# Exponents of a masked decay product in fp32r instead of bf16, in a two-layer attention kernel on one core

## The reference, cut to what matters

```
log_f = log_sigmoid(fg)                       # (8 heads, 128)
cs = cumsum(log_f, axis=1)
log_D = where(tril, cs[:, :, None] - cs[:, None, :], -inf) + ig[:, None, :]
D_mat = exp(log_D - max(log_D, -1))
C = (q k^T / sqrt(32)) * D_mat
h = (C / (max(|sum C|, exp(-max log_D)) + 1e-6)) v
```

## Time and profile before

| what | value |
|---|---|
| median of three runs | 572.49 us (571.02 to 572.50) |
| the profiled execution: time | 568.18 us |
| the profiled execution: span of its trace | 566.5 us |
| TensorE's mean granted clock in it | 0.994 of 2.4 GHz |
| stage A in it | 25.2 to 118.7 us |

### The profile page before, as it was taken

How to read it: one execution, slowest core, us unless ns; L and a number is a source line. 1 busy time by engine, 2 the same in 40 slices (tenths; PEclk the granted TensorE clock), 3 DMA queues, 4 the chain that set the end, 5 groups by cost and what they waited for, 6 DMA issues and landing times.

```text
span 566.5 us, 8464 instructions
## 1 busy us (share of the span) xinstructions
PE 547.5 (97%) x2773; PEld 447.2 (79%) x2773; DVE 326.7 (58%) x799; ACT 230.2 (41%) x436; POOL 71.2 (13%) x105
## 2 busy tenths in 40 slices
PE   7798998999999999899999999999999999999997
PEld 5566576679888888778888878888878889788887
DVE  6677789768877779773353463434552444542333
ACT  2344545647878844362121361122351122441111
POOL 5232324111412323100000000000000000000000
PEclk9998999999999999999999999999999999999999
DMA  7685537334986999200000100000100000000001
GB/s 206 161 199 175 99 105 185 91 118 169 363 303 204 198 318 229 78 1 0 1 0 1 37 2 1 0 1 0 37 1 1 1 1 19 20 1 0 1 0 39
DMA packets 59296, 47.69 MB, mean 84 GB/s; under 512 B 37278, under 2 KB 50590, under 8 KB 58852
## 3 DMA queue, kind: packets, MB, share of 16 engines
q1 hardware_dynamic: 54264, 30.39, 20.1%
q0 software_dynamic: 4848, 16.78, 9.1%
q10 hardware_dynamic: 148, 0.04, 0.0%
HBM read 40.58 MB, written 2.10 MB: 75 GB/s over the span
## 4 chain that ended last, share of the span: by engine, by line
PE 58%; issue 7%; POOL 2%; DVE 1%; POOLq 0%; DVEq 0%
PE ps L914 57%; POOL rstd L445 1%; POOL h L551 1%; PE ps L584 0%; PE ps L878 0%; DVE qr L1527 0%; DVE x L1515 0%; DVE xn L1275 0%; DVE alT L1554 0%; DVE xT L1282 0%; POOL w L540 0%; POOLq L551 0%; POOL w L542 0%; PE ps L869 0%; DVE ot L1607 0%
## 5 line engine op out<-in xcount | busy, mean ns | idle before, releaser
L914 PE MATMUL ps<-hBt,h 128*128 128x512 f32 x512 | 117.5, 390 | 0.0
L914 PE MATMUL ps<-hA,h 128*128 128x512 f32 x512 | 117.3, 390 | 0.0
L1238 ACT ACTIVATE h<-ps,scol 128x512 f32<-128x512 f32 x64 | 44.2, 690 | 175.3 <-PE ps L914 175.2
L914 PEld LDWEIGHTS ps<-hA,h 128*128 128x128 f32 x512 | 95.9, 188 | 20.4 <-DVE hA L1581 0.6
L914 PEld LDWEIGHTS ps<-hBt,h 128*128 128x128 f32 x512 | 95.8, 188 | 20.3 <-DVE hBt L1581 0.6
L914 PE MATMUL ps<-xT,w 128*128 128x512 f32 x256 | 61.7, 396 | 1.0 <-DVE xT L1282 1.0
L914 PEld LDWEIGHTS ps<-xT,w 128*128 128x128 f32 x256 | 46.2, 188 | 15.0 <-issue 6.0
L1599 DVE CAST hBt<-h 128x512 fp32r<-128x512 f32 x32 | 13.7, 427 | 73.7 <-ACT h L1238 73.7
L1599 DVE CAST hA<-h 128x512 fp32r<-128x512 f32 x32 | 13.7, 427 | 70.0 <-ACT h L1238 70.0
L445 POOL TENSOR_TENSOR rstd<-ve,mhalf 128x4 f32<-128x4 f32 x16 | 16.7, 1041 | 262.9 <-DVE ve L1270 262.9
L1221 ACT ACTIVATE silD<-ps,scol 128x512 f32<-128x512 f32 x32 | 22.1, 689 | 45.2 <-PE ps L914 45.2
(11 more groups left out here) (174 smaller groups left out, 877.2 us busy)
## 6 DMA issues: line engine op xcount, KB each, us to landing
looked<-w_all_in SPq DMA_DIRECT2D x16, 704.0 KB, 5.6
h<-w_all_in POOLq DMA_DIRECT2D x16, 512.0 KB, 6.5
V<-ctx_in SPq DMA_DIRECT2D x32, 128.0 KB, 3.4
Qb<-xT SPq DMA_DIRECT2D x64, 64.0 KB, 2.1
w<-w_all_in POOLq DMA_DIRECT2D x3, 1024.0 KB, 7.7
x<-x_in SPq DMA_DIRECT2D x4, 512.0 KB, 4.2
kstA<-ctxT_in SPq DMA_DIRECT2D x4, 512.0 KB, 5.4
kstC<-ctxT_in SPq DMA_DIRECT2D x4, 512.0 KB, 5.8
```

What stands on the lines that cost most here:

```text
L914: last = mm(o, a, b, start=(k == 0 and p == 0), stop=(k == n_k - 1 and p == 1))
L1238: fn(h32[:, m % 2, :], ps[:, 2 + m % 4, :], ACT.Gelu, scale=scol[:, L + 1, m:m + 1])\
```

## The change

The exponent's operands become fp32r, Z is split into two parts in place of three (`ZP = 2`), so that the matmul over them has 10 rows; `gate_c` has two steps. The rows of group parity 1 lie on partitions 32 to 41, those of parity 0 on 0 to 9. The mask's product comes ahead of the one over the rows, and at the start of a group two of them are issued ahead of the wait for the rows. Four DMAs move a group's rows where there were six, with rows of 512 bytes for 256. The constants arrive by five DMAs of GpSimd, which convert bf16 to fp32r, after the gate weights are split; the mask is loaded once and read four times. Nothing behind stage A is touched.

```diff
 RA = 3 + 3 * Q
-MOVES = 16 * 6
+ZP = 2
+RZ = ZP + ZP * Q
+RB = 32
+MOVES = 16 * 2 * ZP
...
-        idb = place(base, "idb", [P, P], BF16)
-        tri = place(base, "tri", [P, Q, S], BF16)
+        idr = place(base, "idr", [P, P], F32R)
+        tri = place(base, "tri", [P, S], F32R)
...
-        Rr = place(a3, "Rr", [RA, 2, Q, 2, Q, S], BF16)
-        Lr = place(a3, "Lr", [RA, 2, 2, Q, S], BF16)
+        Rr = place(a3, "Rr", [RB + RZ, Q, 2, Q, S], F32R)
+        Lr = place(a3, "Lr", [RB + RZ, 2, Q, S], F32R)
...
         def move_rows(sp, u):
-            for part in range(3):
-                sp.dma_start(Rr[part:part + 1, u, :, :, :, :], zp[:, part, 0, :]).then_inc(s["z_moved"], 16)
-                sp.dma_start(Lr[3 + part * Q:3 + part * Q + Q, u, :, :, :], zp[:, part, 1, :])\
-                    .then_inc(s["z_moved"], 16)
+            for part in range(ZP):
+                sp.dma_start(row_of(u, part), zp[:, part, 0, :].bitcast(F32)).then_inc(s["z_moved"], 16)
+                sp.dma_start(columns_of(u, part), zp[:, part, 1, :].bitcast(F32)).then_inc(s["z_moved"], 16)
...
-            for u in range(2):
-                sp.dma_start(Rr[3:RA, u, :, :, :, :], ones_rows_in[3:RA]).then_inc(s["consts"], 16)
-                sp.dma_start(Lr[0:3, u, :, :, :], ones_rows_in[0:3, 0]).then_inc(s["consts"], 16)
-            sp.dma_start(tri[:, :, :], tri_in).then_inc(s["consts"], 16)
...
+            pool.dma_start(tri[:, :], tri_in[:, 0, :]).then_inc(s["rows_ld"], 16)
+            for u in range(2):
+                pool.dma_start(Rr[RB * u + ZP:RB * u + RZ, :, :, :, :], ones_rows_in[3:3 + ZP * Q]).then_inc(s["rows_ld"], 16)
+                pool.dma_start(Lr[RB * u:RB * u + ZP, :, :, :], ones_rows_in[0:ZP, 0]).then_inc(s["rows_ld"], 16)
...
+            def causal(quad):
+
+                mm(ps[:, EX + quad, :], idr[:, :], tri_all, start=True, stop=False)
+
             def expo(g, u, k):
                 q, quad = k // 2, k % 2
                 n = UN * g + k
                 if k == 0:
+                    for a in range(2):
+                        pe.wait_ge(s["d_ready"], n + a + 1)
+                        causal(a)
                     pe.wait_ge(s["z_moved"], MOVES * (g + 1))
-                    pe.wait_ge(s["d_ready"], n + 1)
-                mm(ps[:, EX + quad, :], Lr[:, u, quad, q, :], Rr[:, u, :, quad, q, :],
-                   start=True, stop=False)
-                mm(ps[:, EX + quad, :], idb[:, :], tri[:, :, :], start=False, stop=True)\
-                    .then_inc(s["expo_done"], 1)
+                elif k > 1:
+                    causal(quad)
+                rows = slice(RB * u, RB * u + RZ)
+                mm(ps[:, EX + quad, :], Lr[rows, quad, q, :], Rr[rows, :, quad, q, :],
+                   start=False, stop=True).then_inc(s["expo_done"], 1)
...
             pe.wait_ge(s["gate_copied"], 1)
-            pe.wait_ge(s["consts"], CONSTS)
+            pe.wait_ge(s["rows_ld"], ROWS)
...
                 ch.step(v.tensor_copy(zp[:, 0, :, :], Z[:, :, :]))
                 ch.settle()
-                ch.step(v.tensor_tensor(zr[:, :, :], Z[:, :, :], zp[:, 0, :, :], ALU.subtract))
-                ch.settle()
-                ch.step(v.tensor_copy(zp[:, 1, :, :], zr[:, :, :]))
-                ch.settle()
-                v.tensor_tensor(zp[:, 2, :, :], zr[:, :, :], zp[:, 1, :, :], ALU.subtract).then_inc(s["z_ready"], 1)
+                v.tensor_tensor(zp[:, 1, :, :], Z[:, :, :], zp[:, 0, :, :], ALU.subtract).then_inc(s["z_ready"], 1)
```

More of the change, by code:

```diff
@@ L45 @@
 EPS = 1e-6
-CONSTS = 16 * 10
+A2 = 6
+CONSTS = 16 * 5
+ROWS = 16 * 5
 W_ALL = 2 * KD * HD + MD * D + 2 * MD * HD
@@ L198, in two_layers @@
         a3 = [r2b[0]]
-        Rr = place(a3, "Rr", [RA, 2, Q, 2, Q, S], BF16)
-        Lr = place(a3, "Lr", [RA, 2, 2, Q, S], BF16)
-        gsb = place(a3, "gsb", [2 * NH, GT], F32)
+        Rr = place(a3, "Rr", [RB + RZ, Q, 2, Q, S], F32R)
+        Lr = place(a3, "Lr", [RB + RZ, 2, Q, S], F32R)
+        g3 = [a3[0]]
+        gsb = place(g3, "gsb", [2 * NH, GT], F32)
         NR = NH * Q
-        gi = place(a3, "gi", [NR, S], F32)
-        gf = place(a3, "gf", [NR, S], F32)
-        gb = place(a3, "gb", [NR, 2], F32)
-        fab = place(a3, "fab", [NR, S], F32)
-        fmn = place(a3, "fmn", [NR, S], F32)
-        fl = place(a3, "fl", [NR, S], F32)
-        one_r = place(a3, "one_r", [NR, S], F32)
-        cs = place(a3, "cs", [NR, S], F32)
-        Z = place(a3, "Z", [NR, 2, S], F32)
-        zr = place(a3, "zr", [NR, 2, S], F32)
-        zp = place(a3, "zp", [NR, 3, 2, S], BF16)
-        Er = place(a3, "Er", [NR, S], F32)
+        gi = place(g3, "gi", [NR, S], F32)
+        gf = place(g3, "gf", [NR, S], F32)
+        gb = place(g3, "gb", [NR, 2], F32)
+        fab = place(g3, "fab", [NR, S], F32)
+        fmn = place(g3, "fmn", [NR, S], F32)
+        fl = place(g3, "fl", [NR, S], F32)
+        one_r = place(g3, "one_r", [NR, S], F32)
+        cs = place(g3, "cs", [NR, S], F32)
+        Z = place(g3, "Z", [NR, 2, S], F32)
+        zp = place(g3, "zp", [NR, ZP, 2, S], F32R)
+        Er = place(g3, "Er", [NR, S], F32)
+        assert g3[0] <= r2b[0] + 8 * MB * GT + 16 * GT
         b3 = [r2b[0]]
@@ L234, in two_layers @@
             av_done xC_done d_pre d_sil d_h32 d_hi d_lo d_act d_out xD_done
-            qb0_set ndiag rrs_ready idb_ready dh_own ot_ready dve_prep dve_a2 dve_unit dve_b centred dve_d pool_own act_own out_done pe_own w_ld h1_ld h2_ld""".split()
+            qb0_set ndiag rrs_ready idr_ready rows_ld dh_own ot_ready dve_prep dve_a2 dve_unit dve_b centred dve_d pool_own act_own out_done pe_own w_ld h1_ld h2_ld""".split()
         s = {n: sem(n) for n in names}
@@ L251, in part_made, with row_of, columns_of @@
         def part_made(eng, part):
-            if part < 2:
-                eng.wait_ge(s["dve_a2"], (6, 8)[part])
+            if part == 0:
+                eng.wait_ge(s["dve_a2"], A2)
             else:
                 eng.wait_ge(s["z_ready"], 1)
+        def row_of(u, part):
+            return Rr[RB * u + part:RB * u + part + 1, :, :, :, :].bitcast(F32)
+        def columns_of(u, part):
+            r = RB * u + ZP + part * Q
+            return Lr[r:r + Q, :, :, :].bitcast(F32)
         def move_rows(sp, u):
-            for part in range(3):
-                sp.dma_start(Rr[part:part + 1, u, :, :, :, :], zp[:, part, 0, :]).then_inc(s["z_moved"], 16)
-                sp.dma_start(Lr[3 + part * Q:3 + part * Q + Q, u, :, :, :], zp[:, part, 1, :])\
-                    .then_inc(s["z_moved"], 16)
+            for part in range(ZP):
+                sp.dma_start(row_of(u, part), zp[:, part, 0, :].bitcast(F32)).then_inc(s["z_moved"], 16)
+                sp.dma_start(columns_of(u, part), zp[:, part, 1, :].bitcast(F32)).then_inc(s["z_moved"], 16)
         block = es.enter_context(nc.Block())
@@ L325, in _ @@
                     .then_inc(s["x_rest"], 16)
-            for part in range(3):
+            for part in range(ZP):
                 part_made(sp, part)
-                sp.dma_start(Rr[part:part + 1, 0, :, :, :, :], zp[:, part, 0, :]).then_inc(s["z_moved"], 16)
+                sp.dma_start(row_of(0, part), zp[:, part, 0, :].bitcast(F32)).then_inc(s["z_moved"], 16)
             queries_in(0, 0, 1)
@@ L571, in _ @@
             mm = nc.tensor.matmul
+            tri_all = tri[:, :].rearrange("p (j t) -> p j t", j=1).to_broadcast([P, Q, S])
             pe.sem_inc(s["qk_done"], 4)
@@ L674, in _ @@
             pe.wait_ge(s["gw_lo"], 2)
-            pe.wait_ge(s["idb_ready"], 1)
+            pe.wait_ge(s["idr_ready"], 1)
             gates(0, 0, ctx_first=True)
@@ L1097, in _ @@
             floor_part(0)
-            for part in range(3):
+            for part in range(ZP):
                 part_made(act, part)
-                act.dma_start(Lr[3 + part * Q:3 + part * Q + Q, 0, :, :, :], zp[:, part, 1, :])\
-                    .then_inc(s["z_moved"], 16)
+                act.dma_start(columns_of(0, part), zp[:, part, 1, :].bitcast(F32)).then_inc(s["z_moved"], 16)
             with act.Fori(0, 2) as i:
```

3 lines of the change are left out of this document (1 added, 2 removed).

## The result

The changed kernel takes 585.72 us in the median (6 runs, 578.81 to 587.37), the kernel before in the same session 571.59 us (6 runs, 568.51 to 572.50). The ratio is 1.0227, with a 95% interval from 1.0163 to 1.029. Forecast were 570.0 us, within a range that ended at 576. The kernel is slower, clear of the noise (whether by more than 2% the interval leaves open), and by more than any rival allowed for. One execution each of e12, e15 and e16, and two of the kernel before, stood apart as slow (up to 1600 us): the medians in the table of the experiments count them, the ratios and the clocks do not.

The account below looks back on a forecast made before the run. TensorE, busy 547.5 of 566.5 us, was taken as the bound, with VectorE close in stage A. Terms summed to -1.0, with the clock's -1.5 to -2.5: 572.5 to 570.0 us; range 563 to 576.

Parts of the forecast that it names:

- The lead-in: Before group 0: one part of Z's rows less gives -0.7 us; GpSimd's five added DMA issues hide in its idle time.
- The unit: Stage A on TensorE: exposed fp32r loads make each unit 1.53 for 1.33 us, +6.4 us of work over 32 units.
- The first rival: Stage A's unit on TensorE: both weight loads run ahead, units shrink by 0.18, -9.0 us to 563.5 us; chance 0.20.
- The waits for rows, -2.1: Start of groups 1 and 3: TensorE's waits for Z's rows shrink by 1.2 and 0.9 us, query blocks being next late.
- Splitting Z, -2.3: VectorE in stage A: two steps go, Z is ready 0.76 us sooner three times, -2.3 us where VectorE is the bound.
- the slower rival: Stage A: TensorE becomes the bound everywhere, all 6.4 us lies on the path, +3.6 to 576.1 us; chance 0.20.
- Group 3: Stage A's group that makes no Z: 1.6 us of longer units less its 0.4 of waits for VectorE, +1.2 us.
- The clock, -1.5: TensorE's granted clock in group 1: one of two falls, 1.44 us each, counted as gone, -1.5 us.
- the third rival: Stage A: rows or query blocks still land late, or the clock falls elsewhere, 572.7 us; chance 0.18.

Follow-up runs that it names:

- e12: Changed kernel with GpSimd's five constant transfers issued from 3.6 us and V's setting to ones moved behind the gate weights: 577.77 us, 1.0086 of the kernel before.
- e15: e2 without its two 128 KB transfers, so only the mask's and two of 8 KB stay: 571.57 us, 1.0013 of the kernel before.
- e16: e2 with its two 128 KB transfers spread over 64 partitions in place of 8: 572.32 us, 0.9997 of the kernel before.
- e2: Kernel before with five converting GpSimd transfers added at the change's place, into a tile no engine reads: 576.18 us, 1.008 of the kernel before.
- e9: Changed kernel with GpSimd's five transfers moved behind `inv_root(1)`, about 16 us, and TensorE's wait just ahead of the groups: 583.08 us, 1.0183 of the kernel before.
- e11: e9 with x's two transfers for groups 2 and 3 moved behind Z's rows on SyncE's queue: 577.39 us, 1.0112 of the kernel before.
- e6: Kernel before with rows zero-padded to 128 partitions, their constants loaded by GpSimd from 15.6 us: 568.92 us, 0.9957 of the kernel before.
- e7: e6 with the mask's product first, two of them ahead of the wait for Z's rows: 567.08 us, 0.9922 of the kernel before.
- e3: Kernel before with only the new order: mask's product first, two ahead of the wait for Z's rows: 570.71 us, 0.9986 of the kernel before.
- e8: Kernel before with Z in two bf16 parts, the lowest part left out with its VectorE step and two transfers: 573.45 us, 1.0039 of the kernel before.
- e1: Changed kernel with constants loaded early as fp32 and copied unconverted by GpSimd at the same place: 583.68 us, 1.0213 of the kernel before.
- e10: e9 with the old order, the product over Z's rows ahead of the mask's: 586.48 us, 1.0249 of the kernel before.
- e4: Kernel before with only the mask's product in fp32r, rows in three bf16 parts, old order: 572.08 us, 1.0021 of the kernel before.

## Why the prediction was wrong, point by point

- **The lead-in** is the step that failed: "it idled 5.31 before that, from 9.4 to 14.7, so it hides them", and "Nothing is gained or lost." GpSimd's time was hidden indeed (issues from 10.41 to 13.17). What I did not ask is what the five transfers do to those in flight. They cost 5.1 us in the place of a gain of 0.7. I had even looked at the right queue, but only for issues that it loses. e2 shows 4.1 of the loss without any of the rest of the change, e15 that it is the two large transfers, e9 and e11 that moving them only changes whom they hold up. How they hold V up, whether through the DMA engines or the memory, stays open.
- **The unit** was right in its sum, 1.55 for 1.53, with both loads exposed, and less so in its split. The first rival, loads running ahead, needs one height (e6: 1.17) and the change does not give it. The Trainium skill, "TensorEngine Tiling", key properties, has a change of tiling mode drain the engine. The trace agrees in this, that the unit is longer wherever heights change (1.33 to 1.55) and not in e6 and e7 (1.17, 1.14), where that change is absent; the draining itself is in no row.
- **The waits for rows, -2.1,** were right in themselves (3.7 to 0.8), and wrong in "Next late are the query blocks, which move up by the same 1.3". They were late by 3.8 in all, 2.14 of it in group 1. The term rested on the issue; the landing lies next to that of GpSimd's weight loads, which the prediction had named ("behind other traffic") and left out of the sum. In e3, where neither rows nor blocks moved on the queue, TensorE already waited 2.0 for `Qb`: they had been hidden behind the wait for rows.
- **Splitting Z, -2.3.** VectorE has its 0.76 a group back and TensorE's waits for it are gone (3.8 to 0.3). But TensorE with its longer unit is then the bound, as the slower rival had it: in stage A it is busy 5.24 us more, and 1.94 less of idle time is all that was won against it. e8, with the same shorter chain and the old unit, won 0.7 to 1.5 us at one clock, by the estimate above.
- **Group 3**, which makes no Z, grew from 18.88 to 22.31 us from its first product to stage B. The query blocks account for 1.43, and the clock, 0.92 in it for 1.00 before, for some 1.8. The unit's 1.6 is hardly to be seen: two of the mask's products now stand ahead of the mark, and a wait for VectorE (0.39) is gone.
- **The clock, -1.5.** The sum took one fall as gone, and it is: group 1 has 1.00 where it had 0.87, even behind its wait of 2.14. But groups 2 and 3, which had 1.00, have 0.93 and 0.92:

```profile
52.10:78.81 26.71, 23.82 (x126) 17.47 (x125) 19.95 (x64) 14.46 (x37) 8.89 (x14) 1.00 0.58 132
78.81:104.86 26.05, 25.47 (x126) 18.83 (x126) 20.32 (x59) 12.43 (x33) 9.87 (x15) 0.93 0.50 118
```

  That is about 1.8 us in each, 3.6 for the 3.5 of before, so nothing was won: the falls moved, as the third rival had it ("the clock falls elsewhere"). In group 3 the fall stands 1.3 us behind the wait for the query blocks: the clock is 0.61 from 108 to 109 us and 0.50 from 109 to 110. (The 3.5 of before is nearer two and a half falls of 1.44 than the two of the prediction.) The medians stand further apart than the profiled executions, 14.1 us against 10.6, and here the clock comes in again: the changed kernel's median run has a mean of 0.980 for the profiled one's 0.990 and takes 6.9 us longer. Which part of the change makes it fall more often stays open. In the table the kernels with products of few rows in fp32r stand at 0.978 to 0.989, those in bf16 at 0.988 to 0.996, those with 128 rows everywhere at 0.994 to 0.999; but a late lead-in goes with a low clock too (e9 0.982, e11 0.989 with the same units), and no run changes the clock alone. The 2.2 us behind stage A in the profiled execution are open as well.

Without the lead-in's loss the change would still have been slower. By the profiled executions, 10.6 less 5.1 leaves 5.5 us; e12, with 2.4 of the 5.1 still there, is 5.2 us slower than the kernel before. Both lie above the slower rival's 3.6. No run has the change without any of that loss.

The change's three ideas can be had apart. The order costs nothing once the loads are hidden, and e7 (three bf16 parts, padded rows, mask first) is the fastest kernel here: 567.08 us, 0.9922 of the kernel before and about 3% under the changed one. The padded version with fp32r parts, which would also have the shorter chain, was not run.

## What to carry to other kernels

An idle engine hides the issuing of a transfer, not the transfer: before one is moved, list what is in flight then, what stands behind that on its queue, and who waits at the end; above all for many bytes to few partitions. Where small products stand between large ones, measure from matmul to matmul what each change of height costs; padding with zeros to one height can be cheaper than the small product. And behind each wait that a change removes, the next one has been hiding: look for what is queued behind the thing waited for, and for the traffic that both land with.

## What the runs showed of the hardware

- With five transfers of GpSimd in flight, two of them of 128 KB into 8 partitions, V's four (128 KB each) landed in 6.3 to 7.4 us in place of 4.6 (changed kernel, e1, e2), or x's two (512 KB each) in 7.4 and 7.9 in place of 4.2 (e9, e10), whichever was beside them. Without the two large ones V landed in 4.5 (e15). The queue that issues is held up too: V's issues took 6.34 to 8.92 in place of 3.99, and the one of `gi` 3.04 in the changed kernel in place of 0.85.
- With one height of 128 rows the unit of five matmuls takes 1.14 to 1.17 us (e7, e6), with steps between 15 rows and 128 in bf16 1.33, with one exposed load in fp32r 1.44 and 1.45 (e3, e4), with two 1.55. A bf16 load takes 0.10 us, an fp32r one 0.19.
- A bf16 load behind an fp32r one starts with its own matmul even at one height (e6, e3), without moving it: 0.23 from the matmul ahead.
- In one kernel the mean granted clock and the time go together at 0.6 us (e12) to 0.8 us (e8) for a thousandth, enough to turn the sign of changes of 1 to 3 us.
